# Attention with a linear branch on one NeuronCore: the keys' shift per feature, token tiles transposed by transfers, the values' products in two banks, and the preparing reordered

## The reference

```
xn = (x - mean(x)) / sqrt(var(x) + eps)
# linear attention, 16 heads of 32 features, causal
q, k = elu(xn @ wq) + 1, elu(xn @ wk) + 1 ;  v = xn @ wv
S_t = sum_{i<=t} k_i v_i^T ;  z_t = sum_{i<=t} k_i
lin_t = (q_t S_t) / (q_t . z_t + 1e-6)          ;  out1 = lin @ wo
# softmax attention, 16 heads of 32 features, not causal
Q = xn @ Wq.T + bq ;  K = xn @ Wk.T + bk ;  V = xn @ Wv.T + bv
Qs = (Q/|Q| + query_embedding) * softplus(temperature)
h = softmax(Qs K^T / sqrt(32)) V
# a few gates computed from h scale h, then
out2 = gated(h) @ Wp.T + bp
result = x + out1 + out2
```

## Time and profile before

| | us |
|---|---|
| runs of the kernel | 3869.54, 3873.67, 3873.71 |
| median | 3873.67 |
| the profiled execution | 3873.82 |
| its span in the trace | 3870.4 |
| PE busy | 3708.2 (96%) |
| DVE busy | 3362.6 (87%) |
| ACT busy | 2663.1 (69%) |
| POOL busy | 447.9 (12%) |

### The profile page before, as it was taken

How to read it: one execution, slowest core, us unless ns; L and a number is a source line. 1 busy time by engine, 2 the same in 40 slices (tenths; PEclk the granted TensorE clock), 3 DMA queues, 4 the chain that set the end, 5 groups by cost and what they waited for, 6 DMA issues and landing times.

```text
span 3870.4 us, 147623 instructions
## 1 busy us (share of the span) xinstructions
PE 3708.2 (96%) x65983; PEld 1742.1 (45%) x65984; DVE 3362.6 (87%) x3595; ACT 2663.1 (69%) x2617; POOL 447.9 (12%) x229
## 2 busy tenths in 40 slices
PE   2889999999999999999999999999999999999999
PEld 1544444444444444444444444444444444444433
DVE  5668999899998989889898988889888888888986
ACT  3457777777777677677677677777767767767663
POOL 3101110011101101101110110100110110110120
PEclk8889999999999999999999999999999999999999
DMA  5322212222223313223222323313222221321323
GB/s 208 113 84 61 74 54 63 63 75 61 63 77 90 92 56 115 74 68 98 83 73 82 101 61 92 97 53 104 71 74 68 82 82 46 104 67 56 85 90 106
DMA packets 364210, 315.83 MB, mean 82 GB/s; under 512 B 158168, under 2 KB 312248, under 8 KB 362932
## 3 DMA queue, kind: packets, MB, share of 16 engines
q1 hardware_dynamic: 362852, 297.93, 25.8%
q10 hardware_dynamic: 720, 8.39, 0.5%
HBM read 230.74 MB, written 75.48 MB: 79 GB/s over the span
## 4 chain that ended last, share of the span: by engine, by line
PE 84%; ACT 7%; DVE 4%; issue 3%; SPq 1%; DMA 1%; POOL 0%; ACTq 0%; DVEq 0%; POOLq 0%
PE ps L1098 32%; PE ps L1263 22%; PE ps L1249 19%; ACT prob L924 6%; PE ps L1164 4%; PE ps L1193 2%; PE ps L1133 2%; PE ps L1187 1%; DVE acc L1815 1%; PE ps L1209 1%; SPq L446 1%; PE ps L1072 1%; PE ps L1230 0%; ACT r L868 0%; PE ps L1173 0%
## 5 line engine op out<-in xcount | busy, mean ns | idle before, releaser
L924 ACT ACTIVATE prob<-ps 128x2048 f32<-128x2048 f32 x1024 | 1924.4, 1879 | 604.9 <-PE ps L1249 601.9
L1815 DVE TENSOR_TENSOR acc<-acc,prob 128x2048 f32<-128x2048 f32 x896 | 2057.8, 2297 | 52.5 <-ACT prob L924 37.3
L1263 PE MATMUL ps<-prob,v 128*32 128x512 f32 x8192 | 1091.0, 605 | 0.0
L1249 PE MATMUL ps<-q_hi,k_hi 32*128 32x512 f16 x4096 | 420.0, 384 | 40.6 <-ACT prob L924 35.2
L1098 PE MATMUL ps<-x_hi,w_hi 128*32 128x512 f16 x4096 | 433.4, 383 | 0.4 <-DVE xt_lo L1599 0.4
L1098 PE MATMUL ps<-x_lo,w_hi 128*32 128x512 f16 x4096 | 433.1, 382 | 0.0
L1098 PE MATMUL ps<-x_hi,w_lo 128*32 128x512 f16 x4096 | 432.9, 382 | 0.0
L1249 PE MATMUL ps<-q_hi,k_lo 32*128 32x512 f16 x4096 | 409.9, 374 | 0.8 <-issue 0.8
L1249 PE MATMUL ps<-q_lo,k_hi 32*128 32x512 f16 x4096 | 409.2, 374 | 0.1
L1263 PEld LDWEIGHTS ps<-prob,v 128*32 128x32 f32 x8192 | 161.1, 108 | 433.2 <-issue 433.2
L1098 PE MATMUL ps<-wop_hi,fin 128*32 128x512 f16 x4096 | 348.8, 381 | 4.3 <-DMA y<-in_x 2.6
(11 more groups left out here) (263 smaller groups left out, 4381.6 us busy)
## 6 DMA issues: line engine op xcount, KB each, us to landing
x_hi<-xhi_scratch SPq DMA_DIRECT2D x64, 512.0 KB, 6.2
x_lo<-xlo_scratch SPq DMA_DIRECT2D x64, 512.0 KB, 7.4
x_in<-in_x SPq DMA_DIRECT2D x64, 256.0 KB, 7.1
rq<-rq_scratch SPq DMA_DIRECT2D x64, 256.0 KB
rdl<-rdl_scratch SPq DMA_DIRECT2D x64, 256.0 KB
y<-in_x SPq DMA_DIRECT2D x64, 256.0 KB, 5.9
out<-y SPq DMA_DIRECT2D x64, 256.0 KB, 5.8
rden<-rden_scratch SPq DMA_DIRECT2D x63, 256.0 KB
```

Of the source, the lines that this page charges most:

```text
L924: s_.activation(prob[i % 3][:], ps[:, 0:HG, :], ACT.Exp, bias=-SHIFT, scale=inv_c[:, g:g + 1] if wide else 1.0 / CQK).then_inc(exped, 2)
L1249: last = t_.matmul(bank[h], kk[rows32(h), cols128(kt)], qq[rows32(h), :], start=(kk is kh and qq is qh), stop=(kk is kl and not wide))
L1263: last = t_.matmul(bank[OUT][rows32(h), :], v[m // NB % 2][:, kt, rows32(h)], prob[i % 3][:, h, :], start=(kt == 0), stop=(kt == TT - 1))
L1815: v_.tensor_tensor(acc[:], acc[:], prob[i % 3][:], ALU.add).then_inc(summed, 1)
```

## The change

**1. The keys' shift.** The group that closed every key product is gone, and so are `crow`, `crow_ones` and `rows_of_k`. `mean_k` makes a column of 128 features x 1 (weights stationary), and DVE makes the column `kshift` of it. ACT adds it when it reads the bank: `shift_k` writes k32 (float32) with scale and bias, in slot 2. The hi half is now read from k32 (`split_k`, slot 3), and so is the lo half on DVE (slot 3, behind `normalise`). The squares of k move from slot 3 to 4.

**2. The token tiles.** `turn_x` is gone. ACT and DVE take the halves straight from the normalised x_in, tokens on partitions. They are stored so, and `load_block` reads a block back with `transpose=True`. The sums for the mean are made on POOL for every tile (`xsum`), and PE turns them into a mean once a batch (`mean_x`, 4 matmuls with `ones_s`, slot 7+lag of the steps with the last tile of a batch), with `keep_mean` on DVE behind it. In the opening each tile's halves have a place of their own, so that their splitting doesn't wait for the stores.

**3. The values.** The first half goes to X0, the second to X2. Steps with lag: 18 groups in slot 4, 6 and 3 in slot 5, 9 and 3 in slot 6, 9 in slot 7; before they had 24, 0, 12 and 12. Steps without lag: 24, 9 and 15 in slots 4, 5 and 6. The first half waits for k32 only (X0 read), the second no longer for the first half's reading.

**4. The preparing.** In the prep steps the query of the next block moves from slot 0 of the next step to slot 11, into bank 3, with the reading of it on ACT at slot 12. `turn_dl` stands behind `sum_q`. The splitting of weights stands behind the other work of its slot. In the opening all 16 tiles of x are asked for first, then the constants; the weights' transfers on ACT's queue wait for the first 8 tiles. The norms come at other tiles.

```diff
-                    sp.wait_ge(xt_stored[i], (first + BT) // 2 * 32)
...
-                    sp.dma_start(tile[n % 2][:].rearrange("p t k n -> p t (k n)"),
-                                 src[first:first + BT].rearrange("t p e -> p t e")).then_inc(xb_loaded[n % 2], 16)
+                    sp.dma_start(tile[n % 2][:], src[first * P:(first + BT) * P], transpose=True).then_inc(xb_loaded[n % 2], 16)
...
             def sum_x(t):                                  # POOL, now for all tiles
...
+                if t % TT == 0:
+                    pool.wait_ge(xbar_mm, t // TT)
+                    g_.tensor_copy(xsum[:], xn_of(t)[0]).then_inc(x_summed, 1)
+                else:
+                    g_.tensor_tensor(xsum[:], xsum[:], xn_of(t)[0], ALU.add).then_inc(x_summed, 1)
...
+            act.wait_ge(x_first[1], BT * 16)
             for g in range(NG):
                 act.dma_start(w_raw[g][:], w6_d[g]).then_inc(wraw_in[g], 16)
...
+            def shift_k(n):
+                act.wait_ge(k_proj, n + 1)
+                act.wait_ge(shift_ready, n // NB + 1)
+                act.wait_ge(klo_done, n)
+                s_.activation(k32[:], X0, ACT.Identity, bias=kshift[:, 0:1], scale=KS).then_inc(k_shifted, 1)
+
             def split_k(n):
-                act.wait_ge(k_proj, n + 1)
-                s_.activation(k_hi[n // NB % 2][:, n % NB * BN:(n % NB + 1) * BN], X0, ACT.Copy, scale=KS).then_inc(khi_done, 1)
+                act.wait_ge(k_shifted, n + 1)
+                s_.activation(k_hi[n // NB % 2][:, n % NB * BN:(n % NB + 1) * BN], k32[:], ACT.Copy).then_inc(khi_done, 1)
...
-            def turn_x(t, bk):
-                pe.wait_ge(ln_done, t + 1)
+            def mean_x(b):
+                pe.wait_ge(x_summed, (b + 1) * TT)
                 for k in range(KC):
-                    last = t_.transpose(bk[:, cols128(k)], x_in[t if t < TT else t % 2][:, cols128(k)], ident[:])
-                last.then_inc(x_turned, 1)
+                    last = t_.matmul(X0[:, k:k + 1], xsum[:, cols128(k)], ones_s[:], start=True, stop=True)
+                last.then_inc(xbar_mm, 1)
...
-                by_columns(X0, crow[:], crow_ones[:], False, True).then_inc(k_proj, 1)
+                project(X0, K_, n, range(KC)).then_inc(k_proj, 1)
...
                     if kt == 4 and n is not None:
+                        pe.wait_ge(k_shifted, n + 1)
+                        project_v(n, 0, (whole(0), first(1, 2)) if lag else (whole(0), whole(1)))
+                    if kt == 5 and n is not None:
+                        if lag:
+                            project_v(n, 0, (after(1, 2),))
                         pe.wait_ge(ss_kept, n + 1)
-                        project_v(n, 0)
+                        project_v(n, 1, (first(0, 1 if lag else 3),))
...
+                        pe.wait_ge(v_kept, 2 * n + 1)
+                        if t is not None and t % TT == TT - 1:
+                            mean_x(t // TT)
+                            pe.wait_ge(xbar_ready, t // TT + 1)
                         project(X0, LK_, n, (0, 1))
...
+                    if kt == 11 and n is not None and n + 1 < NB:
+                        pe.wait_ge(qb_done, n + 1)
+                        pe.wait_ge(rdl_kept, n)
+                        query(n + 1)
```

328 lines of the change are left out of this document (167 added, 161 removed).

## The result

The changed kernel takes 3840.46 us (median of 4 runs, 3839.46 to 3848.53), the kernel before 3873.69 us. The ratio is 0.9919 [0.9903, 0.9934]: 33 us faster, where 75 were forecast. The time lies inside the range, near its upper end, but the gain is less than half of what the steps promised.

A forecast was written before the change was run, and what follows sets the result against it. PE was taken to bound steps 16 to 43, with steps 1 to 15 looser and opening and prep steps full of waits. 17.6 + 22.7 + 3.5 - 3 + 13 + 21.1 = 74.9 us off 3873.8 gave 3799 us, range 3775 to 3842.

The forecast's parts named there:

- What bounds the kernel: Steps 16 to 43: PE is busy almost throughout, so its savings of 0.22 + 0.59 us a step show, 22.7 us.
- the light steps: Steps 0 to 15: shortened slots and the values' moved groups save 1.10 us a step, 17.6 us in all.
- The transposing loads: Block loads on SP's queue: the pair may take about 10 us before delaying rden; the sum assumes them as fast as plain.
- the sign of being wrong: Block loads: the forecast is wrong if the pair lands later than 10 us.
- transposing loads are slow: Rival, SP's queue: slow loads delay rden in about 60 steps, 4069 us; near side 3860 to 3900; chance 0.08.
- DVE's spare time: Steps 16 to 43: DVE has 5.6 us a step to spare against 0.8 saved, so it hardly becomes the bound.
- POOL against DVE: Rival, 44 steps: POOL's new sum could cost DVE 1.0 us each by port locking; at most a few us of time.
- Steps 44 to 59: These steps have no token tile; only the keys' closing group goes, 0.22 us each, 3.5 us.
- Opening and prep steps: Ahead of the main steps: the opening gains 13 us (5 to 20), the prep steps 21.1 us.
- half of it is hidden: Rival, light steps, opening and borders: exponential, constants and moved waits hide part; 42 us gained, 3832 us; chance 0.20.

The follow-up runs named there:

- plain loads: Changed kernel with the two transposing loads of a block replaced by plain loads of the same bytes (other data): 3823.86 us.
- late loads: Changed kernel with the next block's pair of transposing loads moved on SP's queue from slot 3 to behind slot 8's transfers, from step -1 on: 3802.31 us.
- Two small edits: Changed kernel with weights' transfers waiting for all constants (3843.94 us), or turn_dl behind the prep steps' key product (3843.93 us); both plus late loads: 3792.26 us.

## Why the prediction was off

**What bounds the kernel.** That PE sets steps 16 to 43, that 0.8 us comes off each, that the light steps lose 1.1 us each: right. The light steps gained 18.1 us for 15.5 forecast; in steps 16 to 43 the undisturbed ones lost 0.83.

**The transposing loads: the step that failed.** The prediction wrote that "the pair may take about 10 us before it delays what stands behind it", from the distance of two issues on SP, 1631.23 and 1641.49. That distance isn't slack. Between them SP issues five other transfers and then sits waiting for rden_c, until 1637.74; SP is free from 1635.0 to 1637.74, and these 2.7 us are the slack. I also priced the loads by their landing, 7.4 us for a plain one, and a landing later than 10 us was to be the sign of being wrong. They land in a median of 7.9 and 5.2 us, well below that. What counts is how long the issue holds the queue: 1.25 us for the pair of the earlier trace rows, a median of 8.0 us now. The excess of 6.8 us against 2.7 of slack makes rden some 4 us late (4.4 in step 19), and DVE's spare time takes part of that. With plain loads 17 us come back. The term that the prediction does not have at all is the second one: loads under way in slots 4 to 6 go with stops of PE, most likely for its own program, 14.9 us of them in steps 16 to 43 and 2.7 with the loads late. The two together, and the clock that falls behind such waits, are the 25.1 us in steps 16 to 43 and 8.5 in 44 to 59 that late loads gave back.

Late loads bring 38 of the 42 us that the change is behind its forecast, but that the sum then comes out within 3 us is in part luck. In the table, opening and prep steps stay 15 us short and steps 16 to 43 stay 5 short, while steps 1 to 15 and 44 to 59 give 5 and 7 us more than forecast.

The rival "transposing loads are slow" had the place and the queue right and the price and the point from which it decides wrong; it had a chance of 8%, and its near side, 3860 to 3900, lay above what came.

**DVE's spare time** was taken as 5.6 us a step. It is an average, and DVE's idle time in these steps hardly changed (158.2 to 164.9 us). Its place did: the wait for kmx went from 9.1 to 41.5 us, that for phkT from 43.5 to 5.8. That this is why a late rden could no longer be made up for is argued and not tested; the kernel before, with transposing loads, waits for rden as well.

**POOL against DVE** was put at "at most a few us". With the loads late it is 11 us: 3.9 in 26 steps, and 6.8 in the two steps with a mean. For such a step +1 us was forecast, for the wait alone; the mean's matmuls take another 1.05 us.

**Steps 44 to 59** lost 0.63 us each where undisturbed (56.56 to 55.93), and 0.22 was forecast. The three groups that moved from slot 6 to slot 5 cost nothing there, since slot 5 had room (2.98 us before, 2.93 now, slot 6 from 3.72 to 3.39). I had counted a group as worth the same in any slot, for which only the light steps' sum was right.

**Opening and prep steps** gave 20.1 us of 35.2. The stop at the constants came where it was forecast, at 38.6 for "near 35", and the first query 9.8 us earlier, for 13 forecast. From the reading of the key in step -4 to that in step -1 it was 99.7 us and is 88.0, 11.7 less for 14.4 forecast (12.0, and 2.4 for closing groups and transposes): the wait ahead of the key moved from qb to dl, 1.25 to 1.23 us and more, and the key's product ran in part at the lower clock, as the border at 122 us shows. From there to the key of step 0 it got 2.2 us longer (42.2 to 44.4), where 3.7 less was forecast. The chain of waits has rq's way through DRAM there, 3.97 and 5.44 us, and not the splits of the weights; no run tried that alone, and the cause of these 6 us stays open. Two small edits and the late loads brought 13.7 us back.

**The direction** was right, faster, and the time lies inside the range, but only since the range took in most of the rival "half of it is hidden" (3832 us). That is luck: the exponential, which was to hide the gain of the light steps, didn't, since these steps gained in full.

## What to carry to other kernels

A transfer has two prices: how long it takes to land, and how long its issue holds the queue that it stands on. Before a kind of transfer is changed, look at what is queued behind it and since when that could have been issued; the slack is the time in which the queue only waits for its next producer (2.7 us here), not the distance to a later transfer (10.3 us). To make a transfer cheap where it stands and to move it are two tests, since a moved transfer takes its traffic along. And an average of an engine's idle time says nothing on the place where a late input meets an in-order program.
